# Bridge and gated convolution of a graph network as one program, on one core

## The chip, the cores and the metric

The kernel runs on one core of a Trainium2 chip. The metric is the device time of one execution in microseconds (us); the median of several runs is given. Engines are named by the profile: PE is TensorE's multiplications and PEld its weight loads, DVE is VectorE, ACT is ScalarE, POOL is GpSimd, SP is SyncE, which here only issues DMAs.

## What is computed

A network on a graph of 3125 nodes (128 features) and 50000 edges sorted by target: three GCN layers (stage L0), a graph attention layer with four heads (L1), a normalisation, a gated edge convolution (L2), a normalisation, then a deep residual GCN of ten layers with a residual branch (L3). The change lies between L1 and L2:

```
x1 = layernorm(x0 + attention(x0) + bias)            # rows: 3125 nodes
z  = concat(x1[dst], x1[src], edge_attr)             # 50000 edges, 3*128
m  = sigmoid(z @ W_f + b_f) * softplus(z @ W_s + b_s)
h  = segment_sum(m, dst)                             # added to x1, then normalised
```

The product with z is split: the first 128 rows of W_f and W_s act on the target node, the next 128 on the source node, the last 128 on the edge's features. So per node there are two tables of 256 columns (128 for f, 128 for s): a **target table** with the bias in it, and a **source table**.

## The kernel before, in words

Everything is in one launch; stages are programs of their own (a `Block`), each engine with its own instruction list, tied by semaphores. At the end of a stage `Semaphores.end` (line 60) clears them behind a barrier of all engines (L62).

**The bridge** (`bridge`, lines 1931 to 2120) goes over the 3125 nodes in seven groups (`GROUPS`): six of four tiles of 125 nodes, one of a single tile. For a group VectorE divides the attention sums by their weights (`normed`: L2068 to L2076), TensorE turns the tiles (`turn`, L1978), VectorE adds bias and residual (`added`, L2084), TensorE centres (`center`, L1986), ScalarE squares (L2025), TensorE averages (`variance`, L1993), ScalarE takes the inverse root as logarithm and exponential (`deviation`, L2030, L2032) and VectorE scales (`scaled`, L2090). `multiply` (L2002) then makes both tables of the group: 8 instructions for the source table, 8 for the target table (an f32 product appears in the trace as two multiplications). ScalarE copies the source table into one of two halves of a staging tile (`sources`, L2039), and SP stores it in DRAM (L1966; 500 KB for four tiles). The target table stays in SBUF as three bf16 parts that add up to the f32 value: VectorE adds the bias (`biased`, L2097), ScalarE casts (`part`, L2044), VectorE subtracts (`rest`, L2102), three casts and two subtractions in turn. The loop is software-pipelined: in step i the engines work on groups i (normalisation), i-2 (tables) and i-3 to i-5 (parts).

**The gated stage** (`gated_conv`, lines 2123 to 2334) goes over 416 pairs (128 edges with one tile of target nodes) in 104 batches of four (`NPB`, `PQ`). For each pair GpSimd gathers 128 rows of the source table from DRAM (L2163, an indirect DMA) into a ring of four slots of a batch each; a slot is free again when VectorE's addition of four batches earlier is done:

```
for b in range(NPB):
    if b >= 4:
        pool.wait_ge(s_zr, b - 3)
    for q in range(PQ):
        pool.indirect_dma_start(xj[:, b % 4, q, :], None, d["p_src"], ...)
```

SP loads, also four batches ahead, the target numbers (L2176) and the edges' features (L2182); before the latter it reads four addresses into registers (`four`, line 1513). TensorE turns the features (`transposes`, L2197), `core` multiplies them and adds the three parts of the target table by one-hot columns (L2208, L2210; it first reads its tile numbers with `four`), VectorE's `add` brings in the gathered rows (L2289), ScalarE makes absolute value, exponential, logarithm (L2257 to L2263) and gate (L2248), VectorE softplus and message (L2295, L2302), TensorE's `scatter` (L2219) sums by target and VectorE adds these sums into `h_t` and `odd` (`merge`, L2311). ScalarE clears `h_t` and `odd` at the start (L2251, L2252). The staging tile, the attention rows and the sums of the bridge had memory of their own; the gather ring lies in `near`, `odd` in `wide`.

The deep layers start when the node sums are complete.

## Time and profile before

| | |
|---|---|
| median of 3 runs | 3440.72 us (3439.77 to 3441.39) |
| span of the profiled execution | 3430.5 us (10.2 us below that median; the page gives no other time for this execution) |
| busy: TensorE, VectorE, ScalarE, GpSimd | 92%, 39%, 40%, 27% of the span |
| bridge | from 1313.7 to 1371.6 us of the span |
| gated stage | from 1372.8 us; deep layers from 1965 us |
| mean granted clock of TensorE | 0.936 of 2.4 GHz |

Times in the rows are microseconds from the start of the span. A busy engine is not necessarily the one that sets the end; what an engine waited for stands in brackets behind its rows.

### The profile page before, as it was taken

How to read it: one execution, taken by the hardware profiler on the slowest of the kernel's cores; microseconds unless marked ns; L12 is line 12 of the kernel's file. 1: busy time of each engine (PE TensorE's matmuls, PEld its weight loads, DVE VectorE, ACT ScalarE, POOL GpSimd, SP SyncE). 2: the span in 40 equal slices, each digit the busy share in tenths (PEclk: the TensorE clock that was granted, in tenths of full speed). 3: DMA queues.
4: the chain of work that ended last, by engine and by line, in shares of the span. 5: the costliest groups of instructions: out<-in, count | busy, mean ns of one | idle time of the engine just before them, and what ended most of it. 6: DMA issues, size and time to landing. Idle time of an engine off the chain costs nothing. (4 is left out here: it accounts for less than half of the span.)

```text
span 3430.5 us, 48040 instructions
## 1 busy us (share of the span) xinstructions
PE 3146.8 (92%) x13945; PEld 2054.3 (60%) x13945; DVE 1342.3 (39%) x3224; ACT 1382.6 (40%) x2450; POOL 910.1 (27%) x935
## 2 busy tenths in 40 slices
PE   5889999969899986798888799999999999999998
PEld 4775555548788875677667555555555555555554
DVE  6991110125656666798888710011110000000012
ACT  4870000224545556777777622222222222222223
POOL 2010000037777760777777500000000000000000
PEclk9999999977867777899999899999999999999999
DMA  1556667623333321666656476666666667766774
GB/s 65 204 204 261 277 286 284 276 58 78 85 80 79 84 57 38 181 179 175 168 164 171 121 292 285 269 269 277 285 287 286 277 276 291 296 281 269 286 301 172
DMA packets 163351, 709.64 MB, mean 207 GB/s; under 512 B 36427, under 2 KB 129482, under 8 KB 150055
## 3 DMA queue, kind: packets, MB, share of 16 engines
q1 hardware_dynamic: 125964, 619.72, 46.0%
q0 software_dynamic: 33920, 84.12, 10.2%
q10 hardware_dynamic: 3224, 2.75, 0.3%
q8 instruction: 130, 2.13, 0.3%
q14 instruction: 113, 0.93, 0.1%
HBM read 658.10 MB, written 48.07 MB: 206 GB/s over the span
## 5 line engine op out<-in xcount | busy, mean ns | idle before, releaser
L1363 PE MATMUL deep_out_psum<-deep_adjacency,deep_scaled_nodes 125*128 125x450 f32 (+1 forms) x1750 | 669.7, 537 | 0.0
L1363 PE MATMUL deep_out_psum<-deep_adjacency,deep_scaled_nodes_odd 125*128 125x450 f32 (+1 forms) x1750 | 669.7, 537 | 0.0
L1601 POOL DMA_INDIRECT source_rows<-gat_source_rows,pair_src x416 | 412.9, 993 | 576.3 <-POOLq L62 449.8
L1363 PEld LDWEIGHTS deep_out_psum<-deep_adjacency,deep_scaled_nodes_odd 125*128 125x128 f32 x1750 | 328.4, 189 | 312.0 <-issue 312.0
L1363 PEld LDWEIGHTS deep_out_psum<-deep_adjacency,deep_scaled_nodes 125*128 125x128 f32 x1750 | 328.1, 189 | 310.7 <-issue 310.7
L2163 POOL DMA_INDIRECT near_room<-gate_source_rows,pair_src x416 | 443.9, 1067 | 231.6 <-issue 125.8
L2208 PE MATMUL gate_core_psum<-edge_weights,edge_features_t 128*128 128x256 f32 x832 | 260.8, 395 | 50.1 <-ACT edge_features_t L2242 49.0
L1421 ACT ACTIVATE deep_squares<-deep_aggregate,deep_vectors 128x450 f32<-128x450 f32 (+1 forms) x70 | 46.7, 668 | 618.0 <-DVE deep_aggregate L1488 618.0
L1363 PE MATMUL gcn_out_psum<-adjacency_columns,gcn_scaled_nodes 125*128 125x450 f32 (+1 forms) x700 | 268.7, 538 | 0.0
L1499 DVE SCALAR_TENSOR_TENSOR deep_normed<-deep_aggregate,deep_vectors,deep_squares 128x450 f32<-128x450 f32 (+1 forms) x70 | 47.9, 684 | 531.8 <-ACT deep_squares L1429 531.8
L2210 PE MATMUL gate_core_psum<-gate_target_rows,gate_node_onehot_t 125*128 x1248 | 206.6, 273 | 0.0
L1363 PEld LDWEIGHTS gcn_out_psum<-adjacency_columns,gcn_scaled_nodes 125*128 125x128 f32 x700 | 131.2, 190 | 123.5 <-issue 122.8
L1427 ACT ACTIVATE deep_squares<-deep_moments,deep_eps 128x450 f32<-128x450 f32 (+1 forms) x70 | 44.4, 634 | 395.4 <-PE deep_moments L1334 395.4
L1639 PE MATMUL score_terms_psum<-ident,source_rows 128*128 128x128 f32 x416 | 149.5, 359 | 43.6 <-DMA source_rows<-gat_source_rows,pair_src 27.2
L1641 PE MATMUL score_terms_psum<-att_node_onehot_t,near_room 125*128 125x128 bf16 x1248 | 189.1, 270 | 0.2
L1488 DVE TENSOR_TENSOR deep_aggregate<-deep_out_psum,dinv_all 128x450 f32<-128x450 f32 (+1 forms) x70 | 43.6, 623 | 348.7 <-PE deep_out_psum L1363 348.7
L507 PE MATMUL adjacency_sum<-h_t,dinv_all 128*128 128x150 f32 x1042 | 161.1, 305 | 19.5 <-DVE h_t L451 18.4
L2208 PEld LDWEIGHTS gate_core_psum<-edge_weights,edge_features_t 128*128 128x128 f32 x832 | 126.2, 192 | 72.8 <-ACT edge_features_t L2242 67.7
L1236 POOL TENSOR_TENSOR identity_branch<-identity_branch,x_t 128x450 f32<-128x450 f32 (+1 forms) x7 | 7.9, 1126 | 605.2 <-ACT identity_branch L1220 605.2
L1689 PE MATMUL pair_sum_psum<-messages,att_node_onehot 128*125 128x132 f32 x800 | 153.2, 351 | 16.4 <-DVE wide_room L1884 14.2
L507 PEld LDWEIGHTS adjacency_sum<-h_t,dinv_all 128*128 128x128 f32 x1042 | 142.3, 194 | 37.5 <-DVE h_t L451 35.3
L2210 PEld LDWEIGHTS gate_core_psum<-gate_target_rows,gate_node_onehot_t 125*128 125x128 bf16 x1248 | 121.7, 98 | 68.1 <-issue 1.6
(404 smaller groups left out, 4553.8 us busy)
## 6 DMA issues: line engine op xcount, KB each, us to landing
deep_adjacency<-adjacency SPq DMA_DIRECT2D x69, 5625.0 KB, 16.3
adjacency_columns<-adjacency SPq DMA_DIRECT2D x19, 5625.0 KB, 16.2
adjacency<-adjacency_columns SPq DMA_DIRECT2D x7, 5625.0 KB, 17.6
edge_features<-in_edge_attr_dram SPq DMA_DIRECT2D x416, 64.0 KB
att_node_rows<-pair_dst_rows SPq DMA_DIRECT2D x104, 125.0 KB
gate_node_rows<-pair_dst_rows SPq DMA_DIRECT2D x104, 125.0 KB
source_rows<-gat_source_rows,pair_src POOLq DMA_INDIRECT x416, 2.5
near_room<-gate_source_rows,pair_src POOLq DMA_INDIRECT x416
```

What stands on the lines that cost most here:

```text
L507: i = nc.tensor.matmul(acc[:, n % BANKS, q * CELLS:(q + 1) * CELLS], ohr[:, n % RING, q, :], cell[:, n % RING, q, :], start=True, stop=True)
L1363: m = nc.tensor.matmul(op[:, n % 2, 0:cols], h[l % 2][:, s, :], ring[0:T, n % 2, s, 0:cols], start=s == 0, stop=s == NS - 1)
L1421: nc.scalar.activation(sq[:, 0:cols], yk, ACT.Square, bias=row[0]).then_inc(s_sq, 1)
L1427: nc.scalar.activation(sq[:, 0:cols], mp[:, 1, 0:cols], ACT.Ln, bias=eps[:, 0:1]).then_inc(s_ln, 1)
L1499: vec.scalar_tensor_tensor(yb[:, 0:cols], yk, vecs[:, l:l + 1], sq[:, 0:cols], ALU.add, ALU.mult).then_inc(s_nm, 1)
L1601: pool.indirect_dma_start(xj[:, b % HOLD, q, :], None, d["h_r"], bass.IndirectOffsetOnAxis(ap=c["pair_src"][:, b * PQ + q:b * PQ + q + 1], ...
L1639: nc.tensor.matmul(o, xj[:, b % HOLD, q, :], c["ident"][:, :], start=True, stop=False, is_transpose=True)
L1641: m = nc.tensor.matmul(o, rows[:, p, bass.ds(tile[q], 1), :].rearrange("r o f -> r (o f)"), oht[:, b % 2, q * 128:(q + 1) * 128], start=Fa ...
L1689: m = nc.tensor.matmul(sums(b)[0:T, q // 2, (q % 2) * SW:(q % 2 + 1) * SW], oh[:, b % 4, q, :], msg[:, b % 2, q, :, :].rearrange("p h f -> ...
L2163: pool.indirect_dma_start(xj[:, b % 4, q, :], None, d["p_src"], bass.IndirectOffsetOnAxis(ap=c["pair_src"][:, b * PQ + q:b * PQ + q + 1], ...
L2208: nc.tensor.matmul(o, e_t[:, b % 2, q * 128:(q + 1) * 128], we[:, :], start=True, stop=False)
L2210: m = nc.tensor.matmul(o, oht[:, b % 2, q * 128:(q + 1) * 128], rows[:, p, bass.ds(tile[q], 1), :].rearrange("r o f -> r (o f)"), start=Fa ...
```

## The change

- `bridge` and `gated_conv` become one program, `bridge_and_gate`; the barrier, the clearing of semaphores and ScalarE's second table load between them go.
- The loop of the bridge makes only source tables. TensorE makes the target tables behind it: group 0 between the last two source groups, groups 1 to 6 after the last source table was copied.
- The bias gets into the target table by a multiplication of a row of ones with the row of biases, ahead of the product into the same PSUM bank, in place of VectorE's addition. The first part is cast straight from PSUM, the second from the rest, the third is written by VectorE as bf16: two casts and two subtractions for a group.
- GpSimd clears `h_t` at the start and `odd` when the last tile is normalised, waits for all stores of the source tables and begins to gather. ScalarE no longer clears.
- SP first loads weights and edges of batches 0 to 3, then stores the source tables, then goes on with batch 4.
- Staging tile, attention rows and sums now lie in `near`, which the gather ring uses later; all PSUM tiles are views of one tensor of eight banks.
- The first transposes and one-hots of the gated stage are done in or behind the bridge's loop; `core(0)` waits for the last part of the last target group.

The diff, cut to its core:

```diff
 def pool:
+            nc.gpsimd.memset(c["h_t"][:, :], 0.0).then_inc(s_cl, 1)
+            pool.wait_ge(s_y, NG_)
+            nc.gpsimd.memset(odd[:, :], 0.0).then_inc(s_cl, 1)
+            for k in range(2):
+                pool.wait_ge(s_st[k], 16 * len(range(k, NG_, 2)))
             for b in range(NPB):
...
 def sp:
+            for b in range(4):
+                edges(b)
+            for g, (s0, n) in enumerate(GROUPS):
+                sp.wait_ge(s_sc, g + 1)
+                sp.dma_start(d["p_src"][...], out[:, g % 2, 0:n, :]).then_inc(s_st[g % 2], 16)
+            for b in range(4, NPB):
+                edges(b)
...
 def pe:
+            def sources(g):
+                pe.wait_ge(s_o, g + 1)
+                if g >= 1:
+                    pe.wait_ge(s_sc, g)
+                for k in range(n):
+                    m = nc.tensor.matmul(p_src[:, k, :], c["x_t"][...], br.w[:, 1, :], start=True, stop=True)
+                m.then_inc(s_ms, 1)
+
+            def targets(g):
+                pe.wait_ge(s_o, g + 1)
+                if g == 1:
+                    pe.wait_ge(s_sc, NG_)
+                if g == 2:
+                    pe.wait_ge(s_o, NG_)
+                if g >= 3:
+                    pe.wait_ge(s_r, g - 2)
+                for k in range(n):
+                    nc.tensor.matmul(p_tgt[g % 3][:, k, :], c["ones"][0:1, 0:T], br.bias[0:1, :], start=True, stop=False)
+                    m = nc.tensor.matmul(p_tgt[g % 3][:, k, :], c["x_t"][...], br.w[:, 0, :], start=False, stop=True)
+                m.then_inc(s_mt, 1)
...
+            turn(0)
+            for i in range(NG_ + 2):
+                if there(i):
+                    center(i)
+                if there(i - 2):
+                    sources(i - 2)
+                if there(i + 1):
+                    turn(i + 1)
+                if there(i):
+                    variance(i)
+                if i == NG_:
+                    targets(0)
             pe.wait_ge(s_wn, 1)
             transposes(0)
             transposes(1)
+            for g in range(1, NG_):
+                targets(g)
+            pe.wait_ge(s_p2, NG_)
             core(0)
...
 def act:
+            def copy_sources(g):
+                act.wait_ge(s_ms, g + 1)
+                if g >= 2:
+                    act.wait_ge(s_st[g % 2], g // 2 * 16)
+                nc.scalar.copy(out[:, g % 2, 0:n, :], p_src[:, 0:n, :]).then_inc(s_sc, 1)
...
+            first_part(0)
             copy_edges(0)
             copy_edges(1)
-            nc.scalar.activation(c["h_t"][:, :], c["ramp"][:, 0:1].to_broadcast([128, N]), ACT.Copy, scale=0.0)
-            nc.scalar.activation(odd[:, :], c["ramp"][:, 0:1].to_broadcast([128, N]), ACT.Copy, scale=0.0).then_inc(s_cl, 1)
+            for g in range(1, NG_ + 1):
+                if there(g):
+                    first_part(g)
+                second_part(g - 1)
...
 def dve:
-            def biased(g):
-                vec.tensor_tensor(full[...], p_m[:, 0, 0:n, :], br.bias[...], ALU.add).then_inc(s_f, 1)
+            def rest(g):
+                dve.wait_ge(s_p0, g + 1)
+                vec.tensor_tensor(left[...], p_tgt[g % 3][:, 0:n, :], rows[:, 0, s0:s0 + n, :], ALU.subtract).then_inc(s_r, 1)
+            def third_part(g):
+                dve.wait_ge(s_p1, g + 1)
+                vec.tensor_tensor(rows[:, 2, s0:s0 + n, :], left[...], rows[:, 1, s0:s0 + n, :], ALU.subtract).then_inc(s_p2, 1)
```

## Rows read from the trace of the kernel before

**Rows 1.** By stretch: us; PE, PEld, DVE, ACT, POOL busy; clock; DMA share, GB/s.

```profile
1325.00:1365.00 40.00, 33.61 (x139) 23.35 (x136) 30.89 (x44) 28.05 (x38) 0.00 (x0) 1.00 0.21 66
1365.00:1389.00 24.00, 4.97 (x17) 3.31 (x18) 6.74 (x11) 11.07 (x14) 11.88 (x13) 0.51 0.51 138
...
1440.00:1584.00 144.00, 130.40 (x888) 104.68 (x887) 129.80 (x251) 113.23 (x139) 111.69 (x107) 1.00 0.67 178
1584.00:1948.00 364.00, 315.68 (x2101) 250.39 (x2099) 309.29 (x591) 267.76 (x328) 280.88 (x260) 0.99 0.59 161
```

**Rows 2.** Timeline of GpSimd: start, duration, instruction, [idle before, releaser].

```profile
1373.47 0.94 POOL L2163 DMA_INDIRECT near_room<-gate_source_rows,pair_src  x1 [105.11 <-POOLq L62]
...
1394.35 0.95 POOL L2163 DMA_INDIRECT near_room<-gate_source_rows,pair_src  x1 [0.30 <-issue]
...
1578.04 0.95 POOL L2163 DMA_INDIRECT near_room<-gate_source_rows,pair_src  x1 [0.30 <-issue]
...
1942.84 0.94 POOL L2163 DMA_INDIRECT near_room<-gate_source_rows,pair_src  x1 [0.30 <-issue]
```

**Rows 3.** Groups by line, 1391 to 2040 us: busy us, mean ns, idle before.

```profile
L2163 POOL DMA_INDIRECT near_room<-gate_source_rows,pair_src x403 | 431.2, 1070 | 122.8 <-issue 122.2 <-DMA near_room<-gate_source_rows,pair_src 0.3 <-DVE wide_room L2289 0.3
```

**Rows 4.** Timeline of VectorE: additions 0, 4, 38 and 103.

```profile
1391.15 1.23 DVE L2289 TENSOR_TENSOR wide_room<-gate_core_psum,near_room 128x1024 f32<-128x1024 f32 x1 [8.40 <-PE gate_core_psum L2210]
...
1409.84 1.23 DVE L2289 TENSOR_TENSOR wide_room<-gate_core_psum,near_room 128x1024 f32<-128x1024 f32 x1 [0.25 <-PE gate_core_psum L2210]
...
1586.22 1.23 DVE L2289 TENSOR_TENSOR wide_room<-gate_core_psum,near_room 128x1024 f32<-128x1024 f32 x1 [0.26 <-PE gate_core_psum L2210]
...
1947.20 1.22 DVE L2289 TENSOR_TENSOR wide_room<-gate_core_psum,near_room 128x1024 f32<-128x1024 f32 x1
```

**Rows 5.** Timeline of TensorE: one iteration of the bridge's loop.

```profile
1334.49 1.11 PE L1986 MATMUL norm_centred<-norm_sum,center_w 128*128 128x500 f32 x2 [0.69 <-DVE norm_sum L2084]
1335.43 3.62 PE L2002 MATMUL gate_tables_psum<-gate_node_weights,x_t 128*125 128x256 f32 x16
1338.88 0.59 PE L1978 MATMUL attention_turned<-ident,attention_rows 125*128 125x125 f32 x4
...
1341.04 1.10 PE L1986 MATMUL norm_centred<-norm_sum,center_w 128*128 128x500 f32 x2 [0.72 <-DVE norm_sum L2084]
```

**Rows 6.** Groups by line and shape, 1313 to 1372 us.

```profile
L2044 ACT CAST gate_target_rows<-gate_target_full 125x1024 bf16<-125x1024 f32 x18 | 18.0, 1038 | 0.8 <-DVE gate_target_full L2097 0.8
...
L2102 DVE TENSOR_TENSOR gate_target_full<-gate_target_full,gate_target_rows 125x1024 f32<-125x1024 f32 x12 | 14.4, 1223 | 3.6 <-ACT gate_target_rows L2044 3.6
```

**Rows 7.** Timeline of SP: all stores, then one; busy time by slice.

```profile
1331.88 35.40 SPq L1966 DMA_DIRECT2D gate_source_rows<-gate_source_stage  x7
...
1352.47 0.25 SPq L1966 DMA_DIRECT2D gate_source_rows<-gate_source_stage  x1
...
1353.00:1354.00 1.00, 0.38 (x2) 0.07 (x1) 0.88 (x2) 0.65 (x1) 0.00 (x0) 1.00 0.23 66
...
1358.00:1359.00 1.00, 0.36 (x2) 0.29 (x2) 1.00 (x2) 0.97 (x3) 0.00 (x0) 1.00 0.05 15
1359.00:1360.00 1.00, 1.00 (x6) 0.88 (x5) 0.43 (x2) 1.00 (x2) 0.00 (x0) 1.00 0.19 53
...
1370.00:1371.00 1.00, 0.00 (x0) 0.00 (x0) 0.62 (x2) 0.96 (x2) 0.00 (x0) 0.50 0.06 23
```

**Rows 8.** Timeline of TensorE: last transposes, start of core 0.

```profile
1384.59 1.11 PE L2197 MATMUL edge_t_psum<-ident,edge_features 128*128 128x128 f32 x4 [2.72 <-DMA edge_features<-in_edge_attr_dram]
1386.23 1.19 PE L2208 MATMUL gate_core_psum<-edge_weights,edge_features_t 128*128 128x256 f32 x2 [0.53 <-issue]
```

**Rows 9.** Groups by line, whole run: GpSimd clears 640 columns.

```profile
L231 POOL MEMSET group_steps<- 128x640 f32 x1 | 0.6, 630 | 0.0
```

**Rows 10.** Timeline of SP: first edge load of batches 2 and 3.

```profile
1382.44 0.37 SPq L2176 DMA_DIRECT2D gate_node_rows<-pair_dst_rows  x1
...
1386.48 0.36 SPq L2176 DMA_DIRECT2D gate_node_rows<-pair_dst_rows  x1
```

More of the change, by code:

```diff
@@ L1957, in bridge @@
+        s_g = [c["sems"].take(f"gate_sources_gathered_{k}") for k in range(4)]
+        s_ed = [c["sems"].take(f"gate_edges_loaded_{k}") for k in range(4)]
+        s_dr = [c["sems"].take(f"gate_node_rows_loaded_{k}") for k in range(4)]
         block = ctx.enter_context(nc.Block())
@@ L2014, in _ @@
                     variance(i)
+                if i == NG_:
+                    targets(0)
+            pe.wait_ge(s_wn, 1)
+            transposes(0)
+            transposes(1)
+            for g in range(1, NG_):
+                targets(g)
+            pe.wait_ge(s_p2, NG_)
+            core(0)
+            for b in range(NPB):
+                if b + 1 < NPB:
+                    core(b + 1)
+                if b + 2 < NPB:
+                    transposes(b + 2)
+                if b >= 1:
+                    scatter(b - 1)
+            scatter(NPB - 1)
         @block.scalar
@@ L2060, in _ @@
+            gate(NPB - 1)
         @block.vector
```

363 lines of the change are left out of this document (157 added, 206 removed).

## Prediction

> **What bounds the kernel now.** I read first the busy time by stretch [rows 1]. The stage that the change rebuilds, the bridge, runs from 1313.7 to 1371.6 us; the gated stage follows and makes its last addition at 1947.2. In the bridge TensorE is busy for 33.6 of 40 us at the full 2.4 GHz; then comes a hole of some 20 us at the lower level, 1.2 GHz (mean grant 0.51). In the gated stage VectorE and TensorE are each busy 85 to 90% of the time, GpSimd 77%, which looks as if the two former set the pace.
>
> GpSimd's timeline says otherwise [rows 2]. Its 416 gathers run from 1373.47 to 1943.78 (1942.84 + 0.94), and before every one shown there is only 0.30 us of issue: it never waited for a free slot. The group's mean [rows 3] is 1.070 us busy, plus 122.8/403 = 0.305 us idle, so 1.37 us for one gather and 5.5 us for a batch of four. VectorE's addition, the reader of each batch, shows two regimes [rows 4]. From batch 4 (1409.84) to batch 38 (1586.22) it advances 5.19 us a batch and waits for TensorE alone. It starts with the gathers some 10 us ahead (batch 4's last ends near 1394.35 + 4 x 1.37 = 1399.8) and eats that up. From there on 65 batches take (1947.20 - 1586.22)/65 = 5.55 us each, the gathers' own pace, with the additions some 3 us behind the last gather. So the end of the stage is set by **the start of the gather stream**: last addition = start of batch 4's gathers (1394.35) + 549.4 (its remaining 400 gathers) + 3.4.
>
> Behind the gated stage nothing is parallel to it: the deep layers need its sums. A shift of its end is a shift of the kernel's.
>
> **The change, part by part.**
>
> *Where batch 4 may start.* The ring has four slots. Batch 4's gathers wait for addition 0 to end. Before, that wait was free: addition 0 ended at 1392.38 and the gathers came round at 1394.35. If the first gathers start much earlier, this wait binds. Therefore two dates are needed: when the sources are stored, and when addition 0 is done. The first can bring 10 us, the second caps it.
>
> *The source half.* An iteration of the old loop lasts 6.55 us [rows 5]: centring at 1334.49, 16 multiplications from 1335.43 to 1338.88 (0.216 us each), turn, variance, next centring at 1341.04. Eight multiplications leave it (1.73 us), as do three VectorE and three ScalarE passes of target work, 1.0 to 1.2 us each [rows 6]. The chain left is 0.94 (centring) + 1.73 (sources) + 0.59 (turn) + 0.7 (the sum on VectorE, for which the centring waits 0.69 and 0.72) + 0.1 = 4.1 us; with normalisation and scaling queued on VectorE I take 4.4. But the stores are slower. A store that moves data alone takes a third of the 16 DMA engines, so a slice of 1 us with a smaller share shows where it begins or ends [rows 7]. The 500 KB store issued at 1352.47 moves data from about 1353.3 (0.23 of 0.33) to 1358.15 (0.05): 4.85 us. Two full ones and the quarter one, back to back, go from 1359.4 to 1370.2: 10.8 us. That is 4.8 for a full one and 1.2 for the small one. In the old loop they hid under 6.55 us. Now they are the pace: the staging tile has two halves, so copy g waits for store g-2. The first is issued at 1331.88, its data begin 0.8 later, at 1332.7, as before; store 4 ends at 1332.7 + 5 x 4.8 = 1356.7, with 0.6 for completion (a choice; no row isolates it) 1357.3; the last copy (0.4) ends at 1357.7; store 6 lands at 1332.7 + 6 x 4.8 + 1.2 + 0.6 = 1363.3. First gather there instead of 1373.47: 10.2 us earlier. Sixteen gathers at 1.37 are done by 1385.2.
>
> *The target half.* Group 0's multiplications fit between sources 5 and 6. Groups 1 to 6 wait for the last source copy, so from 1357.8 TensorE does 21 tiles x 4 multiplications (two for the product, two for the bias) x 0.216 = 18.1 us: 1375.9. The bias multiplication has one partition of contraction, and no row shows such a form. The bounds: nothing, and the 0.216 of the row of the same 256 columns, nearest by shape; I take the row. The Trainium skill ("TensorE: Matmul & The Clock Gate", "Why this matters for your kernels") says that a multiplication over few partitions takes as long as one over 128; by it the sum stays 18.1, and no run here shows it. Two ScalarE casts (2.1 us) and two VectorE subtractions (2.4) per group stay below TensorE's 3.45. The last full group is multiplied at 1375.1. Behind it ScalarE does its cast (1.0), group 4's second part (1.0), the small cast (0.4) and group 5's second part (1.0); then VectorE subtracts for groups 5 and 6 (1.2 + 0.4). With 0.5 for the hand-overs that is 5.5 us: 1380.6.
>
> *Start of the gated stage.* TensorE then reads its tile table and starts core 0. Before, from the second transposes to core 0 passed 1.64 us, from core 0 to addition 0 4.92 [rows 8]. TensorE has idled as it had then, so the clock is low again; as it was warmed a little by transposes then, I add 0.5. Addition 0 starts at 1380.6 + 1.64 + 4.92 + 0.5 = 1387.7 instead of 1391.15, ends at 1388.9; batch 4's gathers start at 1389.05, **5.3 us earlier** than 1394.35. The sixteen first gathers (1385.2) are out of the way. Bounds of this date: -3 us (core 0 warm, tail shorter) to +3.5 (one stretch of slow clock after the wait at 1355, and a slower table read).
>
> *Edits costed at nothing.* The two clears of 3125 columns go from ScalarE, which did them while core 0 ran, to GpSimd. Scaled from the 640-column row [rows 9] they cost about 3 us each; the first is hidden by the bridge, the second starts when the last tile is normalised, near 1340, with 20 us before the first gather. If VectorE waited for the first one, the bridge would start up to 3 us later, though the store pace follows the same shift. SP issues edge loads of four batches (2 + 4 x 5 DMAs, some 4.1 us a batch) ahead of the stores, from 1313.7 on (1386.48 - 1382.44 = 4.04 [rows 10]): done near 1331, the first store is due at 1331.9; a microsecond late at most. The barrier and second table load (1371.6 to 1373.5) vanish; they are inside the dates above. So are VectorE's bias additions and ScalarE's third casts, which fall away.
>
> **Sum.** 3430.5 - 5.3 = 3425.2 for the span. The page gives a span and no time of its own; the median of runs lies 10.2 us above it, and I keep that: 3440.72 - 5.3 = **3435.4 us**.
>
> **Rivals.**
>
> 1. *An earlier addition 0.* If bias multiplications cost nothing, VectorE's 2.4 us a group limits instead of 3.45: 5 us less; or stores go faster with the edge loads away and the target half starts at 1354.9, when the shorter loop alone would allow it: 3 us less. Then the 10.2 us of the first gather become the cap. Gain 8 to 10, time 3431.8. For it: the PE loop is short. Against: the bias product has as many columns as the row that I take. 15%.
>
> 2. *Slower: the target tables at 1.2 GHz.* TensorE falls idle around 1355 for two or three us except for eight transposes, and in rows 1 the hole without its work is low almost throughout. If it stayed low through all 21 tiles, 18.1 us become 36, addition 0 ends at 1407, the kernel takes 3453.5. It decides once 5.3 us of such work are done at the low level, where they take 10.6. Against: before, 40 us with similar work stayed at full clock, and in the gated stage the mean grant is 1.00 again. 5%.
>
> 3. *Gathers held up by VectorE.* During the target half the sixteen gathers run beside the seven second subtractions, which read two SBUF tiles, 6 x 1.22 + 0.4 = 7.7 us in all. Were the gathers stopped for those, they end at 1392.9, batch 4 starts there and the gain is 1.4: 3439.3. Against: the mean of 1.37 already includes a VectorE 85% busy. The Trainium skill ("SBUF — State Buffer", "SBUF: two separate sides") describes an exclusive port pair for which an instruction of one of the two engines waits in full. By that rule the gathers would lengthen as here; no row shows it. 8%.
>
> 4. *The stream's own length changes.* Batches 0 to 37 went at (1578.04 - 1373.47)/152 = 1.346 us a gather, the other 264 at 1.386 [rows 2]. All 400 at the first would end 11 us sooner, all at the second 5 us later. Nothing in the change touches them, but two more us of lead keep the first regime longer (some nine batches, 1.4 us). Gain 16 or 0: 3424.4 or 3440.7. 6% each.
>
> That the change does nothing is excluded: addition 0 cannot stay where it was unless two of my dates fail together.
>
> **How the numbers follow.** Forecast 60%, its own range 3431.5 to 3439. Rival 1 15%, rival 2 5%, rival 3 8%, rival 4 12%. The range 3430.5 to 3441 leaves out rival 2 and most of rival 4's fast half. A measurement of this kernel tells about 0.2%, 6.9 us, from nothing: the forecast lies 1.6 us short of that. About a quarter of the forecast's own weight, rival 1 and half of rival 4 lie beyond it: 0.35 faster; rival 2 and a little: 0.07 slower; 0.58 the same.
>
> **What would show it.** Right: stores back to back at 4.8 us from 1332; first gather near 1363; GpSimd waiting for addition 0 before batch 4, some 4 us; core 0 near 1382; from there 5.2 us a batch, then the gathers' pace. Wrong: last source copy before 1355 (no store pace), a target group of 2.5 us (cheap bias) or 7 us (slow clock), no wait of GpSimd before batch 4, or a stream of 400 gathers off 549 by more than 4 us.

## The result and the profile after

The changed kernel takes **3469.55 us** (median of 4 runs, 3467.0 to 3471.4), the one before 3440.72 beside it (three runs; a fourth took 16116 us, which nothing here explains, and is left out): a ratio of 1.0084, 95% interval [1.0068, 1.0099]. I had forecast 3435.4 with a range up to 3441.0, and gave slower 0.07. It is slower by 28.8 us, and the forecast is wrong in sign.

The busy time by stretch, the columns as in [rows 1]:

```profile
1325.00:1365.00 40.00, 36.44 (x131) 21.97 (x129) 16.50 (x34) 18.99 (x30) 4.85 (x4) 0.93 0.34 110
1365.00:1389.00 24.00, 24.00 (x43) 10.32 (x42) 7.07 (x6) 5.87 (x6) 13.48 (x14) 0.50 0.36 99
1440.00:1584.00 144.00, 128.40 (x853) 101.84 (x854) 125.06 (x242) 108.96 (x134) 113.53 (x101) 0.99 0.63 171
1584.00:1948.00 364.00, 316.41 (x2089) 250.00 (x2088) 306.09 (x586) 266.78 (x327) 284.47 (x262) 0.99 0.61 166
```

In the second stretch, where TensorE had worked 4.97 of 24 us before, it now works all 24, at a grant of 0.50: 1.2 GHz without a gap. Only 43 instructions fit in.

GpSimd's timeline, against [rows 2]:

```profile
1340.37 2.85 POOL L1991 MEMSET wide_room<- 128x3125 f32 x1 [24.62 <-DVE near_room L2230]
1362.39 0.95 POOL L1998 DMA_INDIRECT near_room<-gate_source_rows,pair_src  x1 [19.17 <-DMA gate_source_rows<-near_room]
...
1416.15 1.40 POOL L1998 DMA_INDIRECT near_room<-gate_source_rows,pair_src  x1 [33.70 <-DVE wide_room L2273]
...
1976.43 0.95 POOL L1998 DMA_INDIRECT near_room<-gate_source_rows,pair_src  x1 [0.30 <-issue]
```

The first gather comes at 1362.39, where I had 1363.3. Then, as the forecast said it would, GpSimd stands before batch 4 and waits for addition 0: but for 33.70 us, not 4. The 400 gathers behind that take 1977.38 - 1416.15 = 561.2 us, where before they took 549.4. Two losses, then: a **late start** and a **longer stream**.

TensorE's timeline in the target half shows the first (L2076 brings in the bias, L2077 is the product, L2063 the last source tile, L2085 transposes):

```profile
1353.08 0.70 PE L2077 MATMUL gate_banks<-gate_node_weights,x_t 128*125 128x256 f32 x2
1353.70 0.69 PE L2076 MATMUL gate_banks<-gate_bias,ones 1*125 1x256 f32 x2
1354.33 0.70 PE L2077 MATMUL gate_banks<-gate_node_weights,x_t 128*125 128x256 f32 x2
1354.95 0.69 PE L2076 MATMUL gate_banks<-gate_bias,ones 1*125 1x256 f32 x2
1355.57 0.89 PE L2077 MATMUL gate_banks<-gate_node_weights,x_t 128*125 128x256 f32 x2
1356.26 1.06 PE L2063 MATMUL gate_banks<-gate_node_weights,x_t 128*125 128x256 f32 x2
1357.11 1.91 PE L2085 MATMUL gate_banks<-ident,edge_features 128*128 128x128 f32 x8
...
1362.93 1.21 PE L2076 MATMUL gate_banks<-gate_bias,ones 1*125 1x256 f32 x2
1364.08 1.22 PE L2077 MATMUL gate_banks<-gate_node_weights,x_t 128*125 128x256 f32 x2
1365.22 1.21 PE L2076 MATMUL gate_banks<-gate_bias,ones 1*125 1x256 f32 x2
...
1402.95 1.22 PE L2077 MATMUL gate_banks<-gate_node_weights,x_t 128*125 128x256 f32 x2
1408.80 1.20 PE L2096 MATMUL gate_banks<-edge_weights,edge_features_t 128*128 128x256 f32 x2 [4.63 <-issue]
```

At the full clock a tile (bias and product, four passes) takes 1354.95 - 1353.70 = 1.25 us, 0.312 a pass, where my sum had 4 x 0.216 = 0.86. From 1362.9 on the clock is low and a tile takes 2.29 us. The clock first fell in this work at about 1356, was high again from 1359.4 to 1362.8 and then stayed low until 1414, 10 us behind the last product. TensorE had no idle moment from 1349.3 to 1404. The last product ends near 1404.1; I had 1375.9.

VectorE's timeline has addition 0, and one instruction from the start of the stage that the section on hardware comes back to:

```profile
1313.12 0.71 DVE L2222 TENSOR_TENSOR wide_room<-wide_room 125x528 f32<-125x528 f32 x1
1313.86 1.92 DVE L2224 TENSOR_SCALAR weight_sum<-wide_room 125x16 f32<-125x16 f32 x1
...
1414.65 1.23 DVE L2273 TENSOR_TENSOR wide_room<-gate_banks,near_room 128x1024 f32<-128x1024 f32 x1 [7.54 <-PE gate_banks L2098]
```

### The profile page after: what moved, and what is told of

Read it like the earlier page. It is cut to its first block and busy times, and to the rows that moved or that the text cites. A ratio compares the mean times of both kernels' runs of the same rounds, so it can differ in the third digit from the quotient of the medians.

```text
span 3464.8 us, 48106 instructions
## 1 busy us (share of the span) xinstructions
PE 3198.3 (92%) x13995; PEld 2077.5 (60%) x13995; DVE 1336.9 (39%) x3217; ACT 1371.7 (40%) x2440; POOL 922.9 (27%) x937
## 5 line engine op out<-in xcount | busy, mean ns | idle before, releaser
L1998 POOL DMA_INDIRECT near_room<-gate_source_rows,pair_src x416 | 455.1, 1094 | 179.0 <-issue 126.2
L2096 PE MATMUL gate_banks<-edge_weights,edge_features_t 128*128 128x256 f32 x832 | 263.4, 398 | 51.8 <-ACT edge_features_t L2177 47.0
L2098 PE MATMUL gate_banks<-gate_target_rows,gate_node_onehot_t 125*128 x1248 | 208.3, 275 | 0.0
L507 PE MATMUL adjacency_sum<-h_t,dinv_all 128*128 128x150 f32 x1042 | 162.4, 308 | 18.2 <-DVE h_t L451 17.0
L1689 PE MATMUL pair_sum_psum<-messages,att_node_onehot 128*125 128x132 f32 x800 | 155.6, 355 | 18.7 <-DVE wide_room L1884 15.2
L2096 PEld LDWEIGHTS gate_banks<-edge_weights,edge_features_t 128*128 128x128 f32 x832 | 127.7, 194 | 74.8 <-ACT edge_features_t L2177 64.9
L2098 PEld LDWEIGHTS gate_banks<-gate_target_rows,gate_node_onehot_t 125*128 125x128 bf16 x1248 | 122.7, 98 | 69.3 <-issue 2.8
```

Of the source, the lines that this page charges most:

```text
L507: i = nc.tensor.matmul(acc[:, n % BANKS, q * CELLS:(q + 1) * CELLS], ohr[:, n % RING, q, :], cell[:, n % RING, q, :], start=True, stop=True)
L1689: m = nc.tensor.matmul(sums(b)[0:T, q // 2, (q % 2) * SW:(q % 2 + 1) * SW], oh[:, b % 4, q, :], msg[:, b % 2, q, :, :].rearrange("p h f -> ...
L2096: nc.tensor.matmul(o, e_t[:, b % 2, q * 128:(q + 1) * 128], we[:, :], start=True, stop=False)
L2098: m = nc.tensor.matmul(o, oht[:, b % 2, q * 128:(q + 1) * 128], rows[:, p, bass.ds(tile[q], 1), :].rearrange("r o f -> r (o f)"), start=Fa ...
```

## The experiments

Eighteen runs, e1 to e18, for four questions. They fell on several chips. On chips 0, 8, 13 and 14 the kernel before takes 3437 to 3446 us, as in the first comparison; on chips 6 and 4 it takes 3857 to 3860, because the attention and the gated stage are slower there for every kernel. I call them the first and the second kind, and compare only within a chip, or dates relative to one another within the first kind.

### Is it the bias product over one partition?

e1, e3 and e2 ran on a chip of the second kind. e1 brings the bias rows in through the identity, over 125 partitions, with the same four passes for a tile:

```
- matmul(p_tgt[g % 3][:, k, :], c["ones"][0:1, 0:T], br.bias[0:1, :], start=True, stop=False)
+ matmul(p_tgt[g % 3][:, k, :], c["ident"][0:T, 0:T], br.bias[0:T, :], start=True, stop=False)
```

> The kernel after, with one operand pair exchanged: the target bias comes from the identity (125 x 125) times the bias tile that holds the same row on all 125 partitions, in place of a row of ones (1 partition) times one row. Number, order and columns of the multiplications are the same. Theory A (a multiplication over one partition costs more than its columns say, and a run of them lets TensorE's clock fall to 1.2 GHz although it is never idle): the 21 target tiles take 18 to 20 us instead of 47, addition 0 starts near 1387 instead of 1414.65, the time falls from 3469.5 by about 27 us to some 3442. Theory B (the alternation of two kinds of multiplication, or the missing activity of the other engines, does it): target tiles still 2.29 us each at the low clock, time 3469.

Measured: 3854.92 us against 3860.27 before, ratio 0.9989 [0.9973, 1.0004]; addition 0 at 1669.55 us.

e3 is the changed kernel as it is, beside it:

> The kernel after, unchanged, for a second profile. In the first the 400 gathers from batch 4 on took 561.2 us against 549.4 before. Theory C (the length of the stream is a matter of how gathers and VectorE's instructions happen to fall together in one execution): it differs here from 561.2 by more than 2 us. Theory D (the change lengthens it): within 2 us of 561.2, with some 35 gathers of over 1.5 us against 23 before.

Measured: 3888.16 us (one run), addition 0 at 1694.68. The granted clock in the target half of e1 was 1.00 throughout; in e3 it fell once more and a tile then took 2.29 us. With nothing else changed, the identity brings addition 0 forward by 25.1 us (24.1 when both are counted from VectorE's first instruction of the bridge, 1596.30 in e3 and 1595.28 in e1) and the span by 32.5 (3886.0 to 3853.5). So the loss before addition 0 lies in the form of the bias product. On C and D e3 says nothing: on this chip GpSimd also waits for slots, and the 400 gathers take 688.9 us, in e1 684.5.

e2 leaves the bias out:

```
- matmul(p_tgt[g % 3][:, k, :], c["ones"][0:1, 0:T], br.bias[0:1, :], start=True, stop=False)
- m = matmul(..., start=False, stop=True)
+ m = matmul(..., start=True, stop=True)
```

> The kernel after without the bias multiplications: the gate's bias is left out of the computation. Theory A and B alike: 42 multiplications of 0.216 us in the target half, clock at the high level, and VectorE's two subtractions (2.4 us a group) set the pace; addition 0 near 1383 to 1385, time about 31 us below the kernel after, 3438. If the clock falls here as well, neither the single partition nor the alternation is the cause but the gaps of the target half, and the time stays above 3445.

Measured: 3853.13 us, ratio 0.9981 [0.9966, 0.9996]. The attention stage happened to end 5.7 us earlier than in e1, so I count from VectorE's first instruction of the bridge (1589.57, in e1 1595.28). Addition 0 comes 69.6 us behind it, in e1 74.3. Batch 4's gathers come 75.9 us behind it, in e1 75.8. They no longer wait for addition 0: the sixteen gathers ahead of them now end last, five of them lengthened to 1.96 to 1.99 us beside VectorE's subtractions. So dropping the bias does not bring the stream forward, and the time is e1's within 2 us. The clock was low for 3.4 us from 1634.0, behind a wait of TensorE of 3.0 us, and high in the rest of the target half.

### Slow passes: how many partitions, or the change between them?

These ran on chips of the first kind. e5 is e1 again:

> The bias rows come in through the identity over 125 partitions instead of ones over one partition. Theory A (the one-partition multiplications cost the time: slow passes at either clock, and the clock falls in them): if this chip is like that of the first comparison (kernel before near 3441), a target tile takes 0.87 us, batch 4's gathers start near 1389 and the time is 25 to 34 us under the changed kernel's 3469, so 3435 to 3444, a ratio to before of 0.998 to 1.001. If the gather stream itself is longer by some 12 us in the changed program whatever the tables cost (rival D: placement of buffers or the doubled leads), it ends 12 us later, 3447 to 3456, ratio 1.002 to 1.004, with the 400 last gathers over 558 us.

Measured: 3443.44 us (12 runs) against 3439.76, ratio 1.0007 [0.9997, 1.0017]. TensorE's and GpSimd's timelines of e5:

```profile
1363.16 0.60 PE L2076 MATMUL gate_banks<-gate_bias,ident 125*125 125x256 f32 x2
1363.59 0.60 PE L2077 MATMUL gate_banks<-gate_node_weights,x_t 128*125 128x256 f32 x2
1364.03 0.60 PE L2076 MATMUL gate_banks<-gate_bias,ident 125*125 125x256 f32 x2
...
1374.87 0.59 PE L2077 MATMUL gate_banks<-gate_node_weights,x_t 128*125 128x256 f32 x2
1381.61 1.19 PE L2096 MATMUL gate_banks<-edge_weights,edge_features_t 128*128 128x256 f32 x2 [6.14 <-issue]
```

```profile
1362.23 0.95 POOL L1998 DMA_INDIRECT near_room<-gate_source_rows,pair_src  x1 [19.21 <-DMA gate_source_rows<-near_room]
...
1385.62 0.94 POOL L1998 DMA_INDIRECT near_room<-gate_source_rows,pair_src  x1 [0.30 <-issue]
1388.85 1.39 POOL L1998 DMA_INDIRECT near_room<-gate_source_rows,pair_src  x1 [2.29 <-DVE wide_room L2273]
```

A tile is back at 1364.03 - 1363.16 = 0.87 us, and the dates fall on the forecast's one after the other: last product 1375.46 (1375.9 forecast), core 0 1381.61 (1382.2), batch 4 1388.85 (1389.05). Yet the time is no better than before; the stream of 400 gathers took 565.2 us. That is the last of the four questions.

e7 and e8 use 64 and 65 partitions of ones. The bias is then counted 64 or 65 times in the tables, which changes no timing of an instruction:

```
- matmul(..., c["ones"][0:1, 0:T], br.bias[0:1, :], start=True, stop=False)
+ matmul(..., c["ones"][0:64, 0:T], br.bias[0:64, :], start=True, stop=False)     # e8: 0:65, e16: 0:32
```

> Timing only: the bias comes in over 64 partitions, so it is counted 64 times in the target tables. Theory A1 (few partitions as such are slow, in proportion or below some number of them): a pass between the one-partition cost (0.31 at the full level, 0.57 at the low one) and 0.216, nearer to the latter. Theory A2 (what costs is to switch between operands of few and of 125 or more partitions, since the next weights can then not be loaded beside the running pass): as slow as one partition as long as 64 counts as few, tile 1.25 us at the full level and 2.29 at the low one, with idle issue time ahead of the weight loads.

> Timing only: the bias comes in over 65 partitions, so it is counted 65 times. Theory A1: the same as e7 within 2 per cent. Theory A2, if the limit lies at half of the partitions: a tile of 0.87 us as with the identity, and full clock throughout. If it is neither (a limit elsewhere), e7 and e8 agree and are both fast or both slow.

Measured: 3456.05 and 3444.64 us. TensorE's groups of the two lines from 1350 to 1408 us (busy us, mean ns), first e7:

```profile
L2077 PE MATMUL gate_banks<-gate_node_weights,x_t 128*125 128x256 f32 x50 | 17.4, 430 | 0.0
L2076 PE MATMUL gate_banks<-gate_bias,ones 64*125 64x256 f32 x50 | 17.4, 427 | 0.0
```

then e8:

```profile
L2076 PE MATMUL gate_banks<-gate_bias,ones 65*125 65x256 f32 x50 | 15.0, 380 | 1.1 <-ACT near_room L2161 1.1
L2077 PE MATMUL gate_banks<-gate_node_weights,x_t 128*125 128x256 f32 x50 | 14.9, 379 | 0.0
```

With 64 partitions a tile takes 1.25 us, as with one; with 65 it takes 0.87, as with 125. And not only the bias line is longer but the product, whose operands are the same, by as much (430 against 379 ns). That speaks for A2: the cost lies in going from a product over up to 64 partitions to one over more, and back.

The weight loads (PEld) show what waits. First e7, then e8:

```profile
1366.32 0.29 PEld L2077 LDWEIGHTS gate_banks<-gate_node_weights,x_t 128*125 128x125 f32 x2 [0.33 <-issue]
1366.32 0.70 PE L2077 MATMUL gate_banks<-gate_node_weights,x_t 128*125 128x256 f32 x2
```

```profile
1366.20 0.40 PEld L2077 LDWEIGHTS gate_banks<-gate_node_weights,x_t 128*125 128x125 f32 x2
1366.41 0.60 PE L2077 MATMUL gate_banks<-gate_node_weights,x_t 128*125 128x256 f32 x2
```

With 65 partitions the load starts 0.21 us ahead of its product, beside the one that is running. With 64 it starts no sooner than its product is due; the weight loads stood idle for 0.33 us, and the first load, of 0.18 us, is not hidden.

e12 halves the number of such changes and keeps the columns: one bias product of 512 columns for two tiles.

```
  for k in range(n):
-     matmul(p_tgt[g % 3][:, k, :], c["ones"][0:1, 0:T], br.bias[0:1, :], start=True, stop=False)
+     if k % 2 == 0:
+         w = min(2, n - k)
+         matmul(p_tgt[g % 3][:, k:k + w, :], c["ones"][0:1, 0:T], br.bias[0:1, :] over w tiles, start=True, stop=False)
```

> Bias over one partition still, but one multiplication of 512 columns fills a bank for two tiles, then two products: half as many changes between one-partition and full operands, and the same columns. Theory A2 (each change costs 2 x 0.096 us, since a tile has 2 changes and costs 1.25 instead of 0.86 at the full level): two tiles take 1.73 + 0.39 = 2.1 us at the full level instead of 2.5. Theory A1 (one-partition passes as such are slow): 2.5 still. The clock: if it falls again within the first ten microseconds, one-partition passes bring it down whatever the changes; if it stays up, the stalls at the changes did.

Measured: 3464.07 us. TensorE's timeline of e12 at the full clock:

```profile
1351.73 1.13 PE L2079 MATMUL gate_banks<-gate_node_weights,x_t 128*125 128x256 f32 x4
1352.79 1.12 PE L2078 MATMUL gate_banks<-gate_bias,ones 1*125 1x512 f32 x2
1353.84 1.13 PE L2079 MATMUL gate_banks<-gate_node_weights,x_t 128*125 128x256 f32 x4
```

Two tiles take 1353.84 - 1351.73 = 2.11 us. With two changes instead of four, that is 1.73 (the identity's) plus 0.38; after had 2.50, which is 1.73 plus 0.77. So a change costs **0.19 us at the full clock**, about the length of the load that is no longer hidden, and the few partitions as such cost nothing: A1 falls. The Trainium skill ("TensorE: Matmul & The Clock Gate", "Step-by-step: what each phase is for") says that TensorE loads the next weights beside a running multiplication when the row groups don't conflict, or when the load goes to the background weight buffer. The first condition alone does not draw the line found here: operands over 65 and 128 partitions share rows just as those over 64 and 128 do, and only the latter wait. Why the limit lies there stays open.

### The clock: stalls or few partitions?

In after the clock fell in work without gaps, in e12 at 1359.2, where the only gap since 1348.8 had been one of 0.38 us. e7 has the same stalls as after but 64 partitions; e16 has 32 (on a chip of the second kind):

> Timing only: the bias comes in over 32 partitions, so it is counted 32 times. The passes: 1.25 us a tile at the full level, as with 1 and 64. The clock, theory J (it follows how many partitions are at work): with 1 partition it fell, with 64 it stayed; at 32 either, and the tile says which: 1.25 throughout the target half with addition 0 some 13 us after e5's, or 2.29 with addition 0 some 26 us after. Rival (the fall in the one-partition runs was by chance of the moment): it stays at the full level here and so would one partition in most executions, against three of three so far that fell.

Measured: e16 takes 3885.39 us (3856.90 before), with addition 0 at 1697.6. The target half by stretch, columns as above. e7, 64 partitions:

```profile
1356.00:1364.00 8.00, 8.00 (x34) 4.61 (x33) 0.25 (x1) 2.58 (x4) 0.00 (x0) 1.00 0.35 122
1364.00:1390.00 26.00, 25.52 (x82) 11.75 (x81) 11.05 (x10) 10.22 (x12) 16.09 (x16) 1.00 0.43 125
```

e16, 32 partitions:

```profile
1630.00:1635.00 5.00, 5.00 (x18) 2.43 (x16) 0.00 (x0) 1.01 (x1) 0.00 (x0) 0.95 0.34 119
1636.00:1680.00 44.00, 44.00 (x83) 20.09 (x82) 10.54 (x9) 10.12 (x12) 16.01 (x16) 0.50 0.27 80
```

e12, one partition, half the changes:

```profile
1350.00:1358.00 8.00, 7.62 (x30) 4.13 (x29) 0.54 (x1) 2.88 (x5) 0.00 (x0) 1.00 0.34 118
1360.00:1396.00 36.00, 36.00 (x57) 15.28 (x56) 10.03 (x9) 9.47 (x10) 17.14 (x16) 0.50 0.29 84
```

One partition (after, e3, e12) and 32 (e16) went to 1.2 GHz; 64 (e7), 65 (e8) and 125 (e1, e5 and the four other programs with the identity) stayed at 2.4, the first of them with the stalls of after. So neither idleness nor the stalls brought the clock down; the only thing that differs between after and e7 is the number of partitions of the bias product, and with it how often the bias is counted. For 32, 64 and 65 partitions this rests on one profile each. The two costs can be told apart in dates: from the first gather to addition 0 e5 needs 25.1 us, e7 32.5 (the changes: +7.4, expected 21 x 0.38 = 8.1), after 52.3 (the clock: another 19.8).

### Why is the stream longer?

By the profiles of the first kind of chip (stage = first instruction of the bridge on VectorE to the end of the last gather):

| program | stage, us | last 400 gathers, us | gathers over 1.5 us among them |
|---|---|---|---|
| before; e9; e10 | 630.1; 629.9; 630.5 | 549.4; 549.6; 550.5 | 23; 28; 27 |
| after; e12 | 664.3; 662.4 | 561.2; 566.2 | 35; 42 |
| e5; e8; e7 | 641.2; 641.8; 647.9 | 565.2; 565.9; 564.6 | 41; 42; 39 |
| e17 (e5, start shifted) | 641.1 | 562.4 | 38 |
| e18 (before, start shifted) | 640.1 | 557.2 | 35 |
| e11 (before, softplus split) | 623.0 | 543.0 | 0 |
| e6 (e5, softplus split) | 624.5 | 548.4 | 0 |

e9 and e10 are two more profiles of the kernel before:

> The kernel before, profiled once more. Theory D (the stream of the last 400 gathers is longer in the changed program, 561 to 566 us in four profiles, than in the program before, 549.4 in its one profile): 549 plus or minus 4 again. Rival G (the one profile of before was a quick execution: its span 3430.5 lies 9 us under the runs' median): a stream of 555 to 562 and a span of 3436 to 3442, with the bridge at its old dates relative to the end of the attention stage.

> As e9, a second execution of its own, to see how far two profiles of one program lie apart in the stream and in the attention stage. Theory D: both streams within 4 us of 549.4. Rival G: the streams scatter over some 10 us, and the mean of the three lies near 556.

Measured: 3438.14 and 3441.21 us, with streams of 549.6 and 550.5. The three streams of before lie within 1.1 us, and D stands: in the five unsplit profiles of the changed program and its variants the stream is 11 to 17 us longer. What scatters is the end of the attention stage, 1312.6 to 1321.8 us over twelve profiles. G holds in that alone: the one profile of before ended the attention 6 to 8 us earlier than e9 and e10, and their times lie 1.7 us above their spans, not 10.2.

Where a long gather comes from, two pairs of timelines show. First e9, GpSimd and then VectorE at the third gather of batch 8:

```profile
1425.06 0.95 POOL L2163 DMA_INDIRECT near_room<-gate_source_rows,pair_src  x1 [0.30 <-issue]
```

```profile
1425.16 1.23 DVE L2295 SCALAR_TENSOR_TENSOR gate_core_softplus<-wide_room,gate_core_log 128x1024 f32<-128x1024 f32 x1 [0.17 <-issue]
```

and the same place in e5:

```profile
1413.62 1.85 POOL L1998 DMA_INDIRECT near_room<-gate_source_rows,pair_src  x1 [0.30 <-issue]
```

```profile
1413.43 1.22 DVE L2279 SCALAR_TENSOR_TENSOR gate_core_softplus<-wide_room,gate_core_log 128x1024 f32<-128x1024 f32 x1
```

In e9 the gather starts 0.10 us ahead of the softplus pass and takes 0.95; in e5 it starts 0.19 behind it and takes 1.85. It ends 0.82 behind the softplus, near a plain gather's length behind its end (1415.47 - 1414.65): it waits the pass out. In e5's other cases the same holds: gathers that begin up to 0.03 us behind the start of a softplus pass take 0.95, one that begins 0.05 behind takes 1.99. I put every gather's time over 0.945 us down to what VectorE ran when it began. Nearly all of it falls on passes with two SBUF operands: softplus 30.1 us over some 60 gathers in e9 and 45.3 over 81 in e5, the messages 18.2 and 19.4. The difference in the softplus row, 15.2 us, makes up nearly all of the 15.6 by which e5's stream is longer. The Trainium skill ("SBUF — State Buffer", "SBUF: two separate sides") says that a VectorE pass with two SBUF inputs and a GpSimd instruction that reads SBUF lock each other out, whichever starts first. The held gathers agree with it; the other direction does not show, as the softplus that begins 0.10 us behind a gather's start takes its usual 1.23.

So VectorE's passes of this kind should cost less if they are shorter. e4, e6 and e11 split the softplus pass in two:

```
- scalar_tensor_tensor(sp_[:, :, :], z[...], 0.0, lg[...], max, add)
+ for h in (0, 2): scalar_tensor_tensor(sp_[:, h:h + 2, :], z[.. h:h + 2 ..], 0.0, lg[.. h:h + 2 ..], max, add)
```

e4 is the kernel before with it, on a chip of the second kind:

> The kernel before, with VectorE's softplus (1.22 us, two SBUF operands) cut into two instructions of half the columns. Theory E (a gather that begins while this instruction runs waits for its end: all of the 23 gathers of over 1.5 us began 0.2 us after it): no gather waits more than some 0.6 us, those over 1.5 us vanish, the stream shortens from 549 by 5 to 12 us, time 3430 to 3436. Rival F (long gathers have a cause of their own on GpSimd or in its descriptor ring): still over 20 of them, time 3441 to 3444.

Measured: 3916.86 us, ratio 1.0152 [1.0125, 1.0179], with no gather over 1.5 us. E is right on the gathers and the kernel is slower all the same. GpSimd's group shows where it stands (busy, mean ns, idle by releaser; e4, then e1):

```profile
L2163 POOL DMA_INDIRECT near_room<-gate_source_rows,pair_src x406 | 417.8, 1029 | 461.5 <-DVE wide_room L2289 222.0 <-POOLq L62 135.1 <-issue 104.5
```

```profile
L1998 POOL DMA_INDIRECT near_room<-gate_source_rows,pair_src x416 | 472.6, 1136 | 257.5 <-DVE wide_room L2273 123.8 <-issue 114.3 <-DMA gate_source_rows<-near_room 19.4
```

There GpSimd waits 120 to 220 us for free slots, so the chain of VectorE, ScalarE and TensorE sets the pace on that kind of chip. VectorE's and ScalarE's passes are no slower there (softplus takes 1.22 us in e1 as in e5); the waits between them are longer, TensorE's grant is 0.88 to 0.91 in most of the stage (e15) where before had 0.98 to 1.00, and for much of the waits the trace names no engine of the core. What they wait for stays open. So does the size of e4's loss: the split lengthens VectorE's softplus work by 7.2 us in all (134.0 against 126.8 in e15, the unsplit program), and the stream by 51 (735.8 against 684.6).

e6 (the identity bias and the split) and e11 (before and the split) ran on the first kind:

> e5 and VectorE's softplus pass (two SBUF operands, 1.2 us) in two instructions of 512 columns. Theory E: a gather that begins behind such a pass waits for its end; where the gathers set the pace, shorter passes let more of them through, gathers over 1.5 us fall from some 30 to none and the stream of 400 shortens by 30 x 0.6 to 0.8 = up to 20 us, less what two instructions cost VectorE (104 x 0.06 = 6 us, off the path there). Then 8 to 18 us under e5. Rival: GpSimd gains nothing because VectorE becomes the bound (as in the earlier run on a chip where the gathers waited for it): then GpSimd waits for slots, and the time is e5's or up to 30 us more.

> The kernel before with the softplus pass in two instructions of 512 columns. On a chip where the gathers set the pace theory E gives no gather over 1.5 us and a stream some 10 to 16 us shorter than the unsplit program's, 540 to 549 us; the time 3424 to 3434, ratio 0.995 to 0.998. If what then counts is the start of batch 4 (5.3 us later here than with the joined program), this kernel ends 3 to 7 us behind e6 (3430.2). If E is a coincidence of the joined program, ratio 1.000.

Measured: e6 3430.23 us, ratio 0.9961 [0.9949, 0.9974]; e11 3429.57 us, ratio 0.9970 [0.9961, 0.9979]. Their groups over the last 400 gathers, e6 and then e11:

```profile
L1998 POOL DMA_INDIRECT near_room<-gate_source_rows,pair_src x401 | 427.8, 1067 | 124.3 <-issue 121.0 <-DVE wide_room L2273 3.3
```

```profile
L2163 POOL DMA_INDIRECT near_room<-gate_source_rows,pair_src x402 | 423.3, 1053 | 122.5 <-issue 121.6 <-DVE wide_room L2289 0.9
```

The split is worth 0.4% in the changed program (e6 against e5) and 0.3% in the one before, by 16.8 and 6.6 us of stream. Both beat both kernels on this kind of chip, and e4 warns that on the other kind it costs 1.5%. The joined program still has the longer stream by 5.5 us, so it wins nothing beside e11: the two are level, on two chips, where I had expected e11 3 to 7 us behind.

What sets the pattern of hits? In all five unsplit profiles with the old start (after, e5, e7, e8, e12) the stream reaches batches 8, 12 and 16 at 22.0 to 22.2, 45.7 to 45.8 and 69.9 to 70.0 us; in three of before at 21.6 to 22.0, 42.3 to 42.7 and 64.6 to 65.1. VectorE comes to softplus 4 7.34 us after addition 4 in e5, 7.66 in e9: a shift of 0.3 us, as large as the one between the two orders in the rows above. Theory H was that the start phase decides; e13 to e18 hold batch 4 once until ScalarE has done its absolute values or exponentials of batch 0:

```
  if b >= 4:
      pool.wait_ge(s_zr, b - 3)
+ if b == 4:
+     pool.wait_ge(s_ex, 1)          # e13: s_ab
```

> Identity bias as e5, and GpSimd waits before batch 4, once, also for ScalarE's absolute values of batch 0: the stream starts some 1.1 us later against VectorE's work, all else is the same. Theory H (the phase of the gathers against VectorE's two-operand passes decides how many of them are held up): the pattern of the first 16 batches changes (in e5 batches 8 to 16 take 5.91 and 6.05 us each, seven gathers over 1.5 us up to batch 16), and the stream moves away from 565 by more than 4 us, down most likely, since 565 is the worst seen. Rival I (the layout or order of the changed program lengthens the stream whatever the phase): 563 to 567 again.

> As e13, the wait one step further, for the exponentials of batch 0: some 2.2 us later than e5. Theory H: a third pattern and a third length, 548 to 566, different from e5's by more than 4 us in this run or in e13. Rival I: 563 to 567. Where the stream falls to 550, the span is e5's 3441 less 15 plus 2, near 3428, if the attention stage ends when it did there.

> The kernel before with the same extra wait before batch 4, which shifts the stream by some 1 to 2 us there. Theory H: its first 16 batches no longer follow the three profiles of before (21.8, 42.5 and 64.8 us to batches 8, 12 and 16), and its stream may leave 549.4 to 550.4 by several us, up most likely since those are the shortest seen unsplit. Rival I: 549 to 551 again.

These three fell on a chip of the second kind (3862.89, 3855.20 and 3856.88 us against 3856.90; GpSimd waits 120 to 130 us for slots) and say nothing on the question. Two were repeated on the first kind:

> As e14, on a chip where the gathers set the pace (before near 3441), if it falls so: the identity bias, and batch 4's gathers held once until the exponentials of batch 0 are done, some 2.2 us later than in e5. Theory H (phase): the pattern of the first 16 batches differs from e5's (22.1, 45.7, 70.0 us to batches 8, 12, 16) and the stream leaves 564.6 to 566.0 by more than 4 us. Rival I (layout or order of the changed program, whatever the phase): 563 to 567. On the slower kind of chip: nothing on this question.

> As e15, on a chip where the gathers set the pace, if it falls so: the kernel before, batch 4's gathers held once until the exponentials of batch 0 are done. Theory H (start phase): its stream leaves 549.4 to 550.4 by more than 4 us. Rival I (something else in the program sets it): 548 to 552; the three profiles of before already have batch 4 at 3.2, 1.5 and 2.0 us behind addition 0 and streams within 1 us, which speaks for I. On the slower kind of chip: nothing on this question.

Measured: batch 4 starts 4.2 us after addition 0 in both. The stream of the changed program is 562.4, 2.8 us below e5's: less than H asked for, and within the 561.2 to 566.2 of its profiles with the old start, so e17 shows no effect. That of the program before rises by some 7 to 557.2, which H asked for and rival I ruled out. So in the program before the start phase alone moves the stream by some 7 us (one profile), and no start that was tried brings the changed program to 550. The three profiles of before, whose batch 4 began 3.2, 1.5 and 2.0 us after addition 0, lie within 1.1 us, so the dependence is no smooth one. Why VectorE's softplus comes 0.3 us earlier in some batches of the joined program (4, 8 and 10 in e5) was not found, and no run took that apart. That the longer stream comes of more held gathers is shown; why the changed program has more of them stays open.

## Why the prediction was wrong

**What held.** The chain of the argument: the gathers are the bound, the first gather moves to 1363.3 (1362.39), GpSimd then waits for addition 0, and what counts is the start of batch 4. The stores: back to back, the first issued at 1333.00 (forecast 1331.9); from there to the first gather they took 29.4 us where I had 31.4, so the good date of the first gather comes of two errors that nearly cancel. The last source copy ended at 1357.73 (1357.7), but by luck: in after it waited for TensorE, held up by the bias passes of group 0; in e5 it waited for its store, as forecast, and ended at 1356.87. The 3.4 us from the last gather to the last addition. With the passes priced rightly, as in e5, batch 4 starts 0.2 us from the forecast date.

**The step that failed** is "The bias multiplication has one partition of contraction ... I take the row". A pass costs 0.216 us alone, but beside full products 0.312 at the full clock, so the 84 passes, 18.1 us in my sum, would take 26.3 at the full clock. With the clock low they took 45.2. Together that put batch 4 27.1 us behind its date: some 7.4 by the changes (e7 against e5), 19.8 by the clock (after against e7). My upper bound was the row itself. It had to be higher: no row showed products over different numbers of partitions taking turns, so nothing excluded a cost of the change. The rule of the Trainium skill ("TensorE: Matmul & The Clock Gate", "Why this matters for your kernels") that I set beside it, that few partitions take as long as 128, e12 bears out for the pass itself at the full clock; it says nothing of the change between.

**A second step failed**, "Nothing in the change touches them", of the 400 gathers: the term of 549.4 us measured 561.2 in after and 565.2 in e5. Without the first error alone the forecast would still have missed: e5, with the bias at the price that I had put down, takes 3443.44 us, no gain over before.

**Rival 2** had the right event for the wrong reason and too little weight. I looked for a low clock behind an idle stretch, and gave it 5% because TensorE would be busy. It was busy, and the clock fell. I gave the 21 tiles 36 us and the kernel 3453.5; they took 45.2 (1358.95 to 1404.1), with three of them still near the full clock, as the changes come on top: 2.29 us a tile against 2 x 0.86 = 1.72.

**Rival 4** was right in kind: the stream did change its length, to 561.2. I allowed +5 us for it, from the spread inside one profile. The sum for after: batch 4 +27.1 against the forecast (1416.15 - 1389.05), stream +11.8, what follows +0.7: the 39.6 us between the spans 3464.8 and 3425.2.

**Rival 3** happened in e5 and did not count: four of the first sixteen gathers began inside VectorE's second subtractions and took 1.9 us, and the sixteen ended at 1386.6, ahead of 1388.85. In e2 they are what batch 4 starts behind, so rival 1 had no gain of 8 to 10 us to offer: a still earlier addition 0 left batch 4 where it was. What I called unsupported by a row was in fact the cause of nearly all of the 23 gathers of over 1.5 us already in the trace of before; I had read them as scatter in a mean.

**The term of 10.2 us** from span to median was mis-sized: 1.7 to 2.2 in every other run. The rest was an early end of the attention stage in the one profiled execution. The stage by itself grew by 34.2 us (630.1 to 664.3), and the medians by 28.8. Likewise e5's stage is 11.1 us longer than before's and its median only 3.7. The 5 to 7 us between lie within the scatter of the attention's end, but whether they are only that stays open.

## What to carry to other kernels

A product over few partitions among full ones is not free: over 64 partitions or fewer it costs the change to and fro (0.19 us each here), and over 1 or 32 it brought TensorE to 1.2 GHz in work without gaps. Bring a bias in over the same partitions as its neighbours, through the identity, or add it on another engine. Where GpSimd's gathers set the pace, count as part of them every VectorE pass with two SBUF operands, and try it in shorter pieces: the same pass in two pieces gave 0.3 to 0.4%, and cost 1.5% where the gathers were not the bound.

## What the runs showed of the hardware that was not expected

- TensorE at 100% busy was granted 0.50 for 36 to 44 us (after, e12, e16) with one or 32 partitions in every second or third of its passes, and 1.00 with 64, 65 and 125.
- The limit between slow and quick changes lies between 64 and 65 partitions: 1.25 and 0.87 us a tile. Up to it the next weight load does not go ahead of its product.
- A gather's 0.945 us grows to as much as 1.99 when it starts inside a VectorE pass over two SBUF tiles, and one that starts 0.10 us before it is not touched. The other way round, VectorE's L2224, 0.17 us elsewhere, took 1.92 beside GpSimd's first clear (1313.05 to 1315.75, 2.70 us), in every profile of the changed program, and put the bridge back by 1.75 us. L2222, which began 0.07 us behind the same clear, took its usual 0.71. I had named that wait and given it up to 3 us.
- The same program takes 12% more on some chips, in the attention and gated stages alone, with VectorE's passes of the same length and longer waits between them, and its bound is then another.
